# Two dense mixtures of experts as one block each, the first transfers reordered, and the prefetch blocks removed

## The reference

```python
def _L2_ffn_ref(x, gate_w, w1, w2):
    gate_probs = softmax(x @ gate_w)                  # 8 experts
    top_k_probs, top_k_idx = top_k(gate_probs, 2)
    top_k_weights = top_k_probs / sum(top_k_probs)
    comb = sum(one_hot(top_k_idx, E) * top_k_weights[..., None], axis=2)
    h = gelu(einsum('bnd,edf->benf', x, w1))          # every expert on every token
    expert_out = einsum('benf,efd->bend', h, w2)
    return einsum('bne,bend->bnd', comb, expert_out)

def _L3_ffn_ref(x, w_g, c_fc, c_proj):
    # top 2 of 8 experts by logits, softmax over the two; each expert takes at
    # most cap tokens, first picks before second picks, in order of tokens
    exp_rank = cumsum(exp_mask.reshape(TOP_K * T, N_EXP), axis=0) - 1
    exp_mask = exp_mask * (exp_rank < cap)
    ...
    h = gelu(einsum('ecd,edf->ecf', exp_batches, c_fc), approximate=False)
    exp_out = einsum('ecf,efd->ecd', h, c_proj)
```

## Time and profile before

| | |
|---|---|
| median of 3 runs | 1546.03 us |
| lowest and highest | 1537.41, 1547.57 us |
| the profiled execution | 1545.87 us |
| its span, first to last instruction | 1544.1 us |
| mean granted clock of TensorE | 0.872 of full speed |
| VectorE, ScalarE, GpSimd busy | 47%, 33%, 26% of the span |

### The profile page before, as it was taken

The page is one execution under the profiler, slowest core; times in us unless marked ns, Lnnn a source line. Parts: engine busy times, 40 slices in busy tenths (PEclk is TensorE's granted clock), DMA queues, the critical chain, the costliest instruction groups (busy, mean ns, idle before and its releaser), DMA issues. The chain is left out here.

```text
span 1544.1 us, 26658 instructions
## 1 busy us (share of the span) xinstructions
PE 1289.5 (84%) x10494; PEld 941.2 (61%) x10494; DVE 726.7 (47%) x2167; ACT 512.8 (33%) x1125; POOL 394.2 (26%) x426
## 2 busy tenths in 40 slices
PE   4999477999777757977887799998869999974998
PEld 4868465788533434644564697785547674653776
DVE  4554563444498245653674315526731137654111
ACT  4534132443455313422342212313423324331332
POOL 5930592000433217722760400002010010130000
PEclk9999688999965768988998659998979989895999
DMA  3000402321460000000000000000011100000010
GB/s 128 1 4 1 177 0 70 96 70 29 146 175 1 1 29 1 1 0 1 1 0 1 8 2 1 1 3 1 6 70 41 41 12 1 3 1 28 28 41 27
DMA packets 46543, 48.30 MB, mean 31 GB/s; under 512 B 18944, under 2 KB 37888, under 8 KB 45536
## 3 DMA queue, kind: packets, MB, share of 16 engines
q1 hardware_dynamic: 46432, 46.76, 9.7%
HBM read 41.91 MB, written 4.85 MB: 30 GB/s over the span
## 5 line engine op out<-in xcount | busy, mean ns | idle before, releaser
L976 PE MATMUL bank<-xnT,scratch 128*128 128x512 f32 x256 | 118.0, 610 | 15.2 <-DMA scratch<-e_l_ffn_w 15.2
L1037 DVE SCALAR_TENSOR_TENSOR x_res<-bank,scratch,x_res 128x128 f32<-128x128 f32 x128 | 36.0, 344 | 195.5 <-PE bank L987 195.5
L987 PEld LDWEIGHTS bank<-scratch 128*128 128x128 f32 x1024 | 118.1, 192 | 11.5 <-issue 11.5
L1016 ACT ACTIVATE scratch<-bank 128x512 f32<-128x512 f32 x128 | 76.4, 597 | 143.7 <-PE bank L976 143.7
L987 PE MATMUL bank<-scratch 128*128 128x128 f32 x1024 | 118.2, 275 | 0.0
L976 PEld LDWEIGHTS bank<-xnT,scratch 128*128 128x128 f32 x256 | 48.3, 197 | 67.7 <-issue 66.2
L682 ACT ACTIVATE scratch<-bank 128x512 f32<-128x512 f32 x96 | 52.5, 594 | 92.0 <-PE bank L583 91.9
L641 DVE TENSOR_REDUCE scratch<-bank 128x4 f32<-128x512 f32 x96 | 63.2, 686 | 38.5 <-PE bank L2236 23.0
L2468 PE MATMUL bank<-weights,xnT 128*128 128x512 f32 x64 | 43.9, 788 | 23.6 <-DVE scratch L2577 21.4
L2461 POOL TENSOR_TENSOR scratch<-scratch 128x16 f32<-128x16 f32 x16 | 51.6, 3226 | 39.5 <-DVE scratch L2610 39.5
L647 DVE TENSOR_TENSOR scratch<-bank,scratch 128x512 f32<-128x512 f32 x96 | 61.4, 682 | 0.0
(11 more groups left out here) (529 smaller groups left out, 2845.3 us busy)
## 6 DMA issues: line engine op xcount, KB each, us to landing
scratch<-conv_kernels SPq DMA_DIRECT2D x8, 1024.0 KB, 11.0
scratch<-e_l_ffn_w SPq DMA_DIRECT2D x32, 256.0 KB, 2.8
scratch<-e_l_ffn_w SPq DMA_DIRECT2D x4, 1024.0 KB, 13.5
values<-scratch SPq DMA_DIRECT2D x8, 512.0 KB, 2.8
scratch<-values SPq DMA_DIRECT2D x8, 512.0 KB, 4.3
weights<-w_l_ffn SPq DMA_DIRECT2D x1, 3698.0 KB, 11.7
weights<-w_l_attn SPq DMA_DIRECT2D x1, 2560.5 KB, 8.9
weights<-w_l_attn SPq DMA_DIRECT2D x1, 2048.0 KB, 10.7
```

The source lines that it names most:

```text
L976: nc.tensor.matmul(ps[m % 4][:, :], wa[s][:, i * P:(i + 1) * P], core.xnT[:, half * BANK:(half + 1) * BANK], start=True, stop=True) \
L987: mm = nc.tensor.matmul(ps[4 + half][:, t * P:(t + 1) * P], hT[half][:, i, t * P:(t + 1) * P], wb[s][:, i, :], start=(i == 0), stop=(i == ...
L1016: nc.scalar.activation(hT[half][:, i, :], ps[m % 4][:, :], act_func, bias=bias2[:, s, i:i + 1] if b1 is not None else 0.0) \
```

## The change

1. **Start.** `wo` moves next to `wqT` in `l0_attn`'s weights. SP issues the state space inputs, the first half of those weights (1 MB, `wqT` and `wo`), `x`, the second half, then context, masks, text mask and context tokens. Nothing waits for them in the start block. In `l0_attn` TensorE waits for the first half, VectorE for `x` ahead of the norm, TensorE for the second half ahead of the keys. The mask conversion becomes `take_masks`, in VectorE's stream of `l0_attn` at the end of step 2.
2. **Prefetch.** The load of the next layer's weights is issued by SP between the blocks; the prefetch blocks are gone.
3. **Mixtures.** Norm, scores, routing and experts are one block, and the loop is written out. TensorE turns the normed tokens, makes the scores into bank 7 and goes on to the experts; in `l3_ffn` the counts' matmuls stand after the third up half. Down halves go round three banks (4, 5, 6). VectorE does norm, routing, then the sums, with the context norm ahead of the sum of unit 4. ScalarE loads the gelu's table after the routing's exponential. SP issues the first two experts' weights when the block starts. In `l3_ffn` the exponential's shift takes a maximum of its own (`dve_shift`), so that it doesn't wait for the picks.

```diff
+    def take_masks(self, dve):
+        dve.wait_ge(self.inputs_loaded, 64)
+        self.nc.vector.tensor_copy(self.text_on[:, :], self.text_bytes[:, :])
+        self.nc.vector.tensor_scalar(self.key_bias[:, :], self.mask_bytes[:, 0:B * P], 1.0, FAR, ALU.subtract, ALU.mult)
+        self.nc.vector.tensor_scalar(self.lat_key_bias[:, :, 0:P], ...)
...
+class Route:
+    BANK_OF_SCORES = 7
+    def pe(self, pe):
+        for b in range(B):
+            mm = self.nc.tensor.matmul(self.scores()[:, b * 8:(b + 1) * 8], self.core.xnT[:, b * P:(b + 1) * P], self.wr,
+                                       start=True, stop=True)
+        mm.then_inc(self.scored.sem, self.scored.up())
+    def act(self, act):
+        act.wait_ge(self.shifted.sem, self.shifted.at(0))
+        self.nc.scalar.activation(self.prob, self.prob, ACT.Exp).then_inc(self.exped.sem, self.exped.up())
+    def dve_shift(self, dve, link):
+        nc, scores = self.nc, self.by_batch(self.scores())
+        dve.wait_ge(self.scored.sem, self.scored.at(0))
+        link(nc.vector.tensor_reduce(self.col, scores, AX_X, ALU.max))
+        nc.vector.tensor_tensor(self.prob, scores, over_experts(self.col), ALU.subtract) \
+            .then_inc(self.shifted.sem, self.shifted.up())
...
+class RouteWithCapacity(Route):
+    def pe_counts(self, pe):
+        pe.wait_ge(self.picked.sem, self.picked.at(0))
+        for k in range(2):
+            self.nc.tensor.matmul(self.scores(k), self.tri, self.picks[k].rearrange("p b e -> p (b e)"),
+                                  start=True, stop=False)
+            mm = self.nc.tensor.matmul(self.scores(k), self.core.ones[:, :],
+                                       self.before[k].rearrange("p b e -> p (b e)"), start=False, stop=True)
+        mm.then_inc(self.counted.sem, self.counted.up())
...
+def mixture(core, tag, c, w1, w2, act_func, route, aside=None):
+    UNITS, COUNTS_AT, ASIDE_AT = 2 * E, 2, 4
+    UP_BANKS, Y_BANKS = (0, 1, 2, 3), (4, 5, 6)
...
+            for h in range(2):
+                norm.pe(pe, h, Y_BANKS[h])
+            pe.wait_ge(*core.w_loaded[tag])
+            pe.wait_ge(x_out.sem, x_out.at(1))
+            route.pe(pe)
+            for u in range(UNITS + 1):
+                if u < UNITS:
+                    up(u)
+                if u == COUNTS_AT:
+                    route.pe_counts(pe)
+                if u > 0:
+                    down(u - 1)
...
+            core.load_table(ACT.Exp)
+            act.wait_ge(norm.turned.sem, norm.half(norm.turned, 0))
+            nc.scalar.copy(core.xnT[:, half(0)], ps[Y_BANKS[0]][:, :]).then_inc(x_out.sem, x_out.up())
+            route.act(act)
             core.load_table(act_func)
...
+            norm.dve(dve)
+            dve.wait_ge(norm.turned.sem, norm.half(norm.turned, 1))
+            dve.wait_ge(x_out.sem, x_out.at(0))
+            nc.vector.tensor_copy(core.xnT[:, half(1)], ps[Y_BANKS[1]][:, :]).then_inc(x_out.sem, x_out.up())
+            route.dve(dve)
+            dve.wait_ge(route.done.sem, route.done.at(0))
+            for u in range(UNITS):
+                if u == ASIDE_AT and other is not None:
+                    other.dve(dve)
+                dve.wait_ge(down_made.sem, down_made.at(u))
...
-    wqT, wk, wvT, wo = w.take(CH, P), w.take(CH * P), w.take(CH, P), w.take(CH, D)
+    wqT, wo, wk, wvT = w.take(CH, P), w.take(CH, D), w.take(CH * P), w.take(CH, P)
...
-            pe.wait_ge(*core.w_loaded[tag])
+            pe.wait_ge(core.first_loaded, 16)
...
             pe.wait_ge(x_out.sem, x_out.at(0))
+            pe.wait_ge(*core.w_loaded[tag])
             keys(0)
...
+            dve.wait_ge(core.x_loaded, 16)
             norm.dve(dve)
...
+                if s == 2:
+                    core.take_masks(dve)
...
                 sp.dma_start(core.ssm.inputs, ssm_in).then_inc(core.ssm.loaded, 16)
-                sp.dma_start(core.x[:, :, :], x_in.rearrange("b s d -> s b d")).then_inc(loaded, 16)
...
-                load_weights(sp, 0)
-                sp.dma_start(core.ctxk[:, :, :], ctxk_in.rearrange("b s d -> s b d")).then_inc(loaded, 16)
-                sp.wait_ge(loaded, 80)
+                sp.dma_start(wbuf[0][:, 0:FIRST], weights[names[0]][:, 0:FIRST]).then_inc(core.first_loaded, 16)
+                sp.dma_start(core.x[:, :, :], x_in.rearrange("b s d -> s b d")).then_inc(core.x_loaded, 16)
+                sp.dma_start(wbuf[0][:, FIRST:first_width], weights[names[0]][:, FIRST:]).then_inc(buffer_loaded[0], 16)
...
             if n + 1 < len(names):
-
-                with nc.Block(f"{name}_prefetch", no_gpsimd_drain=True) as block:
-
-                    @block.sync
-                    def _(sp):
-                        load_weights(sp, n + 1)
+                load_weights(nc.sync, n + 1)
```

More of the change, by code:

```diff
@@ L940, in mixture @@
[L940 to L943, removed]
+    half = lambda h: slice(h * BANK, h * BANK + BANK)
+    x_out, up_made, up_out, down_made, added = (core.count(n) for n in (
+        "x_out", "expert_up", "expert_act", "expert_down", "expert_added"))
@@ L957, in _ @@
         @block.gpsimd
         def _(pool):
-            for h in range(2 if aside is not None else 0):
-                aside.pool(pool, h)
+            for h in range(2):
+                norm.pool(pool, h)
+            if other is not None:
+                pool.wait_ge(norm.xn.sem, norm.batch(norm.xn, B - 1))
+                for h in range(2):
+                    other.pool(pool, h)
         @block.tensor
         def _(pe):
[L964 to L971, removed]
-                for i in range(HC):
[L973 to L978, removed]
@@ L989, in down @@
[L989 to L997, removed]
+                        mm = nc.tensor.matmul(ps[Y_BANKS[u % 3]][:, t * P:(t + 1) * P], hT[h][:, i, t * P:(t + 1) * P],
+                                              wb[e % 2][:, i, :], start=(i == 0), stop=(i == HC - 1))
+                mm.then_inc(down_made.sem, down_made.up())
@@ L1002, in _ @@
+            act.wait_ge(norm.turned.sem, norm.half(norm.turned, 0))
+            nc.scalar.copy(core.xnT[:, half(0)], ps[Y_BANKS[0]][:, :]).then_inc(x_out.sem, x_out.up())
+            route.act(act)
             core.load_table(act_func)
[L1003 to L1018, removed]
+            for u in range(UNITS):
+                if u >= 2:
+                    act.wait_ge(down_made.sem, down_made.at(u - 2))
+                for i in range(HC):
+                    act.wait_ge(up_made.sem, up_made.at(u * HC + i))
+                    nc.scalar.activation(hT[u % 2][:, i, :], ps[UP_BANKS[i]][:, :], act_func) \
+                        .then_inc(up_out.sem, up_out.up())
@@ L1020, in _ @@
         @block.vector
         def _(dve):
[L1022 to L1040, removed]
@@ L1120, in layer_l2_ffn @@
[L1120 removed]
+    mixture(core, tag, c, w1, w2, ACT.Gelu_apprx_tanh, Route(core, tag, c, w),
+            aside=core.ctxk)
 def layer_l3_ffn(core, tag, w, w1, w2):
[L1126 to L1128 removed]
     c = Carve(core.scratch)
[L1130 to L1132 removed]
@@ L1192, in layer_l3_ffn @@
-    mixture(core, tag, c, w1, w2, ACT.Gelu, gates)
+    mixture(core, tag, c, w1, w2, ACT.Gelu, RouteWithCapacity(core, tag, c, w))
 def layer_l0_ffn(core, tag, w, w1, w2):
```

222 lines of the change are left out of this document (107 added, 115 removed).

## The result

| | kernel before | kernel after |
|---|---|---|
| median, on the same chip | 1541.72 us (4 runs) | 1501.04 us (4 runs) |
| lowest and highest | 1537.1, 1547.57 us | 1500.23, 1503.95 us |
| the profiled execution, its span | 1545.87, 1544.1 us | 1500.95, 1499.2 us |
| mean granted clock of TensorE | 0.872 | 0.880 |

The ratio of the times is 0.9738, with an interval of 0.9693 to 0.9782: 2.6% less time. The forecast of 1501.0 was made against the profiled execution, and between the two profiled executions the spans differ by 44.9 us, which is the sum forecast. That agreement to a tenth is luck, and it rests on an execution of the kernel before that was slower than its median: by the medians the saving is 40.7 us. The terms measure 9.1 (start), 6.3 (ten seams), 10.1 (l2_ffn) and 18.6 (l3_ffn), and 0.8 that nobody forecast in l0_attn; their misses, up to 1.7 us, cancelled.

A forecast was written before the change was run, and what follows sets the result against it. The expert loop was taken as bound by TensorE's matmul passes, which the change leaves alone; gains of 8.9 + 8.0 + 10.1 + 17.9 = 44.9 us off 1545.9 gave 1501.0, range 1489 to 1510.

The forecast's parts named there:

- Start, 8.9 forecast: At the start, l0_attn's norm begins when x lands at 8.8 instead of at 17.71: 8.9 us gained (3.0 to 9.7).
- Seams, 8.0 forecast as 10 x 0.80: Between layers, dropping prefetch blocks cuts VectorE's idle from 1.22 to 0.42 us, ten times: 8.0 us (0 to 9).
- l2_ffn, 10.1 forecast: In l2_ffn, TensorE goes straight from scores, ending at 1128.4, to expert 0, which began at 1138.55: 10.1 us gained.
- l3_ffn, 17.9 forecast: In l3_ffn, experts follow scores directly, 18.8 us, less 0.9 for counts among expert matmuls: net 17.9 us (15.9 to 18.8).
- Unrolling, 0 forecast: At the expert loop's turns, TensorE's passes already touch, so writing the loop out gains 0.
- Clock, 0 forecast: In both mixtures, scores running into experts bring no sooner clock rise: 0, at most 2.5 in l3_ffn, 2.0 in l2_ffn.
- the prediction's own signs of being wrong: TensorE idle inside units 0 to 3, expert 0's weights landing after scores, or a changed clock in a mixture's first 10 us.
- The clock gives more back: Rival: with shorter pauses TensorE may stay warm, l3_attn's opening passes giving 5 us, 1494 in all; chance 0.15.
- `x` at 8.5: Rival at the start: behind its megabyte x lands at 13 and not 8.8, giving 1505; chance 0.08.
- the seams gone: Rival at the ten boundaries: a DMA between blocks is still met by all engines, nothing saved, 1509; chance 0.07.
- the clock up in both mixtures: Slower rival: the clock does not come up in a mixture; one whole mixture cold gives 1613; chance 0.02.
- the picks in time: Rival in l3_ffn: the picks are late by more than the slack, costing 3 us, 1504; chance 0.05.

The follow-up runs named there:

- control: The kernel after run once more with nothing changed: 1505.33 us by the median of 4, ratio 0.97.
- h_scores_later: Kernel after with expert 0's first up half ahead of the scores in both mixtures, counts at 3, extra table changes: 1500.12 us, ratio 0.9688.
- h_gates_first: Kernel after, but TensorE does the counts and waits for the gates ahead of expert 0: 1519.5 us.

## Why the prediction was right

**The total** was right, with the mechanism it named: TensorE's work did not change and its idle stretches went. By its steps:

- **Start, 8.9 forecast.** Measured 17.71 - 8.57 = 9.1. With the start put back but one meeting left out, the norm moves by 8.1 and the stage by 8.9. `x` was reckoned to land at 8.8 and landed at 1.63 + 6.9 = 8.5. The bound of 14.7 by x's own pace was rightly left aside. The second half of the weights landed at 2.10 + 9.4 = 11.5 (its own time to landing; the 7.5 of the row is the median of the two halves), forecast 12.0, and was covered as said. The keys began 5.1 after the norm and not 5.9, because TensorE's first products, which stand ahead of the turns of the normed tokens and began with the norm before (17.71), now begin 0.8 ahead of it, at 7.77. The forecast had kept the 5.9. Read at the keys the gain is 9.95, and this is where l0_attn could give more than was forecast. Its net 0.8 also holds the paces of the passes, which change between executions. Masks: nothing, as said.
- **Seams, 8.0 forecast as 10 x 0.80.** The seam itself measured 0.39 against 1.22, and 1.19 with the blocks put back, so the price was right. Between the two profiled executions the ten stages show 6.3 (l3_attn's clock and l1_ffn took some back, l2_attn gave 2.4); the experiment on the whole says 8.9, for eleven blocks and with a control on another chip. Six of the ten changed by 0.77 to 0.89 each, as the seam alone would have it (l3_xattn's is what the last stage lost, 19.47, less l3_ffn's 18.58). What the forecast left out is that a stage's clock can answer to the seam: in l3_attn the 0.8 saved came with a longer stretch at the low clock.
- **l2_ffn, 10.1 forecast.** The stage fell by 10.93, of which 0.83 is its seam: 10.1. The experts begin 1111.84 - 1102.15 = 9.7 after the block's start, forecast 9.8. The gelu's table was ready when reckoned: first gelu 2.2 after the scores' end, 2.4 forecast. The weights' slack, forecast 1.4, was 0.8 to 1.0.
- **l3_ffn, 17.9 forecast.** Measured 18.6. The counts took 1395.29 - 1394.45 = 0.84, forecast 0.9; the picks took 10.8 from the scores' end, forecast 11.2; the slack was 4.4, forecast 2.9, or 5 from a cold start. The 0.7 left over is the first 16 passes, 8.59 for 9.40.
- **Unrolling, 0 forecast.** Shown by a kernel of its own, ratio 0.999.
- **Clock, 0 forecast.** This step was mis-sized in l3_ffn. "The scores last only 3.55" was taken to mean that running them into the experts brings nothing; it brought 0.8 there, in each of six profiles (8.59 to 8.62 against 9.40, 9.63 and 9.91 behind a pause). In l2_ffn it brought nothing: 8.79 to 9.34 in those same six, against 8.85, 9.09 and 9.39 with a pause. This also made one of the prediction's own signs of being wrong come true: the clock in the first 10 us of l3_ffn did differ from before.

**The rivals.** "The clock gives more back" named l3_attn, and there it did not happen: the pause went to 1.56 us, the clock still stood at 0.53 over 1228 to 1235, and the stage grew by 1.2. The others were seen not to hold: `x` at 8.5, the seams gone, the clock up in both mixtures, the picks in time.

**Still open.** l3_attn took 88.1 us after and 87.0 before, although its seam got 0.8 shorter. This follows the prefetch blocks. The three profiles with them show 86.96, 86.99 and 87.11 us (before, blocks back, loop written out), and six of the seven without them 88.12 to 88.68. The first stretch at the low clock is as long before as after, 13.7 us. The second is 3.4 us in the three profiles with the blocks and 6.8 in those six without. What starts and ends that second stretch no run shows, nor whether it can be avoided while the seam stays short. In the seventh, h_scores_later, the first stretch was 10.2 us, the second 3.4, and the stage took 84.9. Nor do the runs say why the scores bring the clock up sooner in one mixture and not in the other.

## What to carry to other kernels

Price a change like this by the idle time of the bounding engine, stage by stage, and check each stage against its own term: single executions of the control lay up to 8.0 us apart, while the two mixtures and the start came within 0.7 of their terms. Work of another engine costs nothing as soon as it lies beside the bounding stream, and what then decides is how far the stream can run before it must wait (4.4 us here for the picks, 0.8 for the weights): measure that slack, since the next change uses it up. A block that holds a single issue costs all engines a meeting.

## What the runs showed of the hardware

**A busy TensorE may be held at the low clock for very different times in the same code.** l2_xattn took 70.3, 71.6 and 75.0 us in kernels that share it. Two stretches at the same place of that stage, the kernel after and then h_gates_first, both with TensorE busy throughout:

```profile
1051.80:1071.80 20.00, 20.00 (x177) 11.92 (x175) 14.40 (x28) 8.80 (x17) 0.00 (x0) 0.85 0.01 2
```

```profile
1051.40:1071.40 20.00, 20.00 (x129) 10.98 (x128) 9.21 (x19) 5.87 (x11) 0.00 (x0) 0.58 0.01 1
```

177 passes at a mean clock of 0.85, 129 at 0.58. The 4.7 us between the shortest and the longest are more than half of this forecast's smallest term, and they fell in a stage in which these kernels have the same code.

**An issue can hold SP.** SP's load of the next layer's weights took 1.78 us at 7.74, with the first transfers not yet landed (1.17 to 2.00 in the other profiles with the new start), and 0.33 to 0.35 at every later seam. With the old start, where all had landed, it took 0.33 at 16.60. In the kernel after it was free, since nobody waits for SP; with a prefetch block around it (1.49 us there) l0_attn opened 2.0 us later.
